# The router's logits: tokens streamed past 32-column weights, then a 32x32 transposition on VectorE

## The reference

```python
logits = hidden @ router_w.T                 # [8192, 128] @ [128, 16]
top_vals, top_idx = jax.lax.top_k(logits, K) # K = 1
scores = sigmoid(top value at its expert, 0 elsewhere)
routed_in = hidden[None, :, :] * scores.T[:, :, None]
```

## Time and profile before

| | |
|---|---|
| device time, median of 3 runs | 510.09 us (509.06 to 510.21) |
| span of the profiled execution | 528.1 us |
| TensorE busy | 497.9 us, 94% |
| VectorE busy | 363.4 us, 69% |
| ScalarE busy | 345.9 us, 66% |
| POOL busy | 347.9 us, 66% |

### The profile page before, as it was taken

One profiled execution on the slowest core, in us unless ns is written; L12 is line 12 of the kernel. 1 busy time (PEld: TensorE's weight loads), 2 busy tenths in 40 slices (PEclk: granted clock), 3 DMA queues, 4 the chain that ended last, 5 costly groups with the idle time before them and its releaser, 6 DMA issues.

```text
span 528.1 us, 10518 instructions
## 1 busy us (share of the span) xinstructions
PE 497.9 (94%) x3101; PEld 406.0 (77%) x3101; DVE 363.4 (69%) x1036; ACT 345.9 (66%) x643; POOL 347.9 (66%) x576
## 2 busy tenths in 40 slices
PE   8889999999999999999999999999998998799984
PEld 7646777877877877878577679888887987799874
DVE  5978889889889889888787888446434433444335
ACT  3777897987987988977789775632534534455321
POOL 6766668778778778785887866635154565556660
PEclk9999999999999999999999999999999899999988
DMA  6015001101101101101010010102877434441009
GB/s 219 2 51 209 20 21 41 60 22 41 60 21 42 60 22 42 50 11 62 12 50 21 21 41 32 41 21 72 204 207 189 137 101 125 129 116 49 30 12 308
DMA packets 33031, 39.32 MB, mean 74 GB/s; under 512 B 4913, under 2 KB 29113, under 8 KB 32720
## 3 DMA queue, kind: packets, MB, share of 16 engines
q1 hardware_dynamic: 26640, 24.97, 16.2%
q0 software_dynamic: 5760, 13.16, 7.2%
q10 hardware_dynamic: 576, 0.52, 0.3%
HBM read 21.68 MB, written 17.93 MB: 75 GB/s over the span
## 4 chain that ended last, share of the span: by engine, by line
PE 61%; DVE 7%; ACT 7%; issue 7%; another core or an unknown queue 7%; POOL 6%; DMA 2%; SPq 1%; ACTq 0%; DVEq 0%; POOLq 0%
PE bank L418 14%; PE bank L411 8%; PE bank L435 4%; PE bank L405 3%; PE bank L426 3%; PE bank L704 2%; PE bank L705 2%; PE bank L534 2%; PE bank L520 2%; PE bank L544 2%; PE bank L530 2%; PE bank L525 2%; PE bank L551 2%; PE bank L577 2%
## 5 line engine op out<-in xcount | busy, mean ns | idle before, releaser
L418 PE MATMUL bank<-hT,wm 128*128 128x256 f32 x512 | 128.7, 390 | 3.4 <-ACT hT L821 2.2
L418 PEld LDWEIGHTS bank<-hT,wm 128*128 128x128 f32 x512 | 94.0, 195 | 21.8 <-ACT hT L821 7.2
L1287 POOL DMA_INDIRECT out<-shared x55 | 53.9, 979 | 47.3 <-DVE shared L1136 32.2
L411 PEld LDWEIGHTS bank<-wm,k 128*128 128x128 f32 x512 | 62.3, 192 | 10.7 <-issue 6.9
L411 PE MATMUL bank<-wm,k 128*128 128x128 f32 x512 | 63.7, 277 | 1.2 <-ACT k L838 0.9
L870 ACT ACTIVATE er<-bank 128x256 f32<-128x256 f32 x40 | 15.2, 383 | 54.9 <-remote 33.1
L1141 DVE TENSOR_TENSOR e<-er,bank 128x256 f32<-128x256 f32 x40 | 16.8, 420 | 31.1 <-ACT er L870 20.3
L1287 POOL DMA_INDIRECT out<-rows x24 | 23.5, 978 | 20.5 <-DVE rows L1136 11.3
L799 ACT ACTIVATE h<-rows,smE 128x128 f32<-128x128 f32 x64 | 26.3, 482 | 12.6 <-POOL smE L1231 12.5
L435 PE MATMUL bank<-wm,actA 128*128 128x128 f32 x240 | 32.8, 280 | 0.0
L435 PEld LDWEIGHTS bank<-wm,actA 128*128 128x128 f32 x240 | 29.3, 192 | 0.2
(11 more groups left out here) (258 smaller groups left out, 1401.6 us busy)
## 6 DMA issues: line engine op xcount, KB each, us to landing
shared<-sorted_rows SPq DMA_DIRECT2D x56, 128.5 KB
shared<-x SPq DMA_DIRECT2D x16, 256.0 KB
rows<-sorted_rows SPq DMA_DIRECT2D x24, 128.5 KB
wexp<-w_exp SPq DMA_DIRECT2D x2, 1536.0 KB, 9.6
sorted_rows<-filler SPq DMA_DIRECT2D x17, 128.5 KB
shared<-out SPq DMA_DIRECT2D x6, 256.0 KB
out<-shared SPq DMA_DIRECT2D x12, 128.0 KB, 2.3
sorted_rows<-rows,posi POOLq DMA_INDIRECT x64
```

Source lines behind the costliest of these rows:

```text
L411: ins = mm(grp(acc, g), grp(lhs, g), W(name, f), start=(f == 0 and g == 0), stop=(f == F // P - 1), skip_group_check=True)
L418: ins = mm(dst[:, j * HALF:(j + 1) * HALF], W(name, 2 * pair_ + j), src[:, half * HALF:(half + 1) * HALF], start=True, stop=True)
L1287: g_.indirect_dma_start(out, bass.IndirectOffsetOnAxis(xr[k % RING][:, j, D:D + 1].bitcast(U32), 0), xr[k % RING][:, j, D + 1:ROW], None, ...
```

## The change

- The router's weights are padded from 16 to RW = 32 columns with zeros (on the host), and become the loaded operand.
- Per tile there are 4 matmuls as before, now one for each quarter c of the array's columns. Each loads the same 128x32 weights into its own 32 columns, streams 128 tokens past them (from each of the 4 groups the 32 tokens c*32 to c*32+31) and writes the PSUM partitions c*32 to c*32+31. The result LGT has 128 partitions (quarter and expert) by 128 columns (group and token).
- VectorE transposes LGT in blocks of 32x32 into `lgt` in SBUF. There a token is again on its own partition, with 4 groups of 32 logits, of which 16 are real.
- mx and oh0 read lgt in SBUF in place of LG in PSUM. mx waits for the transposition.

```diff
-               ("router", NE), ("gate", SF), ("up", SF), ("down", SF)):
+               ("router", RW), ("gate", SF), ("up", SF), ("down", SF)):
...
+        lgt = ring("lgt", 2, (G, RW))
...
-        LG = SMALL[:, 0:G * NE].rearrange("p (g e) -> p g e", e=NE)
-        RK5 = SMALL[:, G * NE:(2 * G + 1) * NE].rearrange("p (g e) -> p g e", e=NE)
+        LGT = SMALL[:, 0:P]
+        RK5 = SMALL[:, P:P + (G + 1) * NE].rearrange("p (g e) -> p g e", e=NE)
...
-                    for g in range(G):
-                        ins = mm(LG[:, g, :], grp(hT[t % HR], g), W("router"), start=True, stop=True)
+                    tokens = hT[t % HR][:, :].rearrange("p (g c i) -> p c g i", g=G, c=P // RW)
+                    for c in range(P // RW):
+                        ins = mm(LGT[c * RW:(c + 1) * RW, :].rearrange("e (g i) -> e g i", g=G), W("router"),
+                                 tokens[:, c, :, :], start=True, stop=True)
                     ins.then_inc(s["LG"], 1)
...
                     wait(dve, "LG", t)
+                    v.transpose(lgt[t % 2][:, :, :].rearrange("p g e -> p (g e)"), LGT).then_inc(s["lgt"], 1)
+                    wait(dve, "lgt", t)
                     wait(dve, "ths", t - 2)
-                    v.reduce_max(mx[t % 2][:, :], LG, AX).then_inc(s["mx"], 1)
+                    v.reduce_max(mx[t % 2][:, :], lgt[t % 2][:, :, 0:NE], AX).then_inc(s["mx"], 1)
...
-                    v.tensor_tensor(oh0[t % 2][:, :, :], LG, mx[t % 2][:, :].unsqueeze(2).to_broadcast([P, G, NE]),
+                    v.tensor_tensor(oh0[t % 2][:, :, :], lgt[t % 2][:, :, 0:NE], mx[t % 2][:, :].unsqueeze(2).to_broadcast([P, G, NE]),
                                     ALU.is_equal).then_inc(s["oh0"], 1)
```

More of the change, by code:

```diff
@@ L38 @@
 LN_EPS, WKV_EPS = 1e-5, 1e-8
+RW = 32
 ROW = 2 * D + 1
@@ L70 @@
     kr2=1, k22=1, VAL2=1, K3=1, kr3=1, k23=1, VAL3=1, REC=1, th=1, rv=1, x2=1, agE=2, pE=3, h=1, T4=1,
-    hT=1, LG=1, mx=1, oh0=1, cm=2, oh=1, ths=1, sc=1, hs=1, RK=1, prk=1, reg=1, pmk=1, posf=1,
+    hT=1, LG=1, lgt=1, mx=1, oh0=1, cm=2, oh=1, ths=1, sc=1, hs=1, RK=1, prk=1, reg=1, pmk=1, posf=1,
     posi=1, G0=1, U0=1, sg0=1, ac0=1, G1=1, U1=1, sg1=1, ac1=1, D1=1, base=1, hG0=1, hU0=1, hsg0=1, hac0=1,
@@ L1314 @@
         "Wkey": a["attn_Wkey"].T, "Wrec": a["attn_Wrec"].T, "Wval": chunks(a["attn_Wval"].T),
-        "router": a["ffn_router_w"].T, "gate": a["ffn_shared_gate_w"].T, "up": a["ffn_shared_up_w"].T,
+        "router": np.pad(a["ffn_router_w"].T, ((0, 0), (0, RW - NE))), "gate": a["ffn_shared_gate_w"].T, "up": a["ffn_shared_up_w"].T,
         "down": chunks(a["ffn_shared_down_w"].T),
```

## The result

The change makes the kernel slightly slower. The changed kernel takes 514.09 us (median of 6 runs, 512.25 to 514.3), the kernel before, run in turn with it, 509.97 (6 runs, 509.06 to 510.48). The ratio of the runs is 1.0058, with a 95% interval of 1.0035 to 1.0081: some 3 us, with 1.8 and 4.1 as the ends of the interval. The forecast was 512.4.

A forecast was written before the change was run, and what follows sets the result against it. A closed loop through VectorE (stA to reciprocal), POOL and the x load was taken as the bound. +2.2 us in 8 turns and +0.1 in three later tiles, +2.3 on 510.09, gave 512.4 us, range 508.0 to 516.0.

The forecast's parts named there:

- Rival 1: TensorE is the real pace maker and gains: 507.2 us, or 503.6 with the larger saving; chance 0.14.
- The transposition: On VectorE between stA and the reciprocal L1093: adds 0.32 us a tile, bounds 0.20 and 0.93.
- Nothing comes back: On VectorE, reduce_max and the first comparison save no time by reading SBUF in place of PSUM.
- The turn: From stA to stA, 8 times: tight turn 20.16 becomes 20.48 us; 8 x 0.27 = +2.2 us in all.
- TensorE: the failed term: Router matmuls and changes of array shape on TensorE: 0.85 us in place of 0.81, +0.04 a tile.
- the third sum: Router matmuls on TensorE overlap only in program order: 5 slots of 0.11, 0.55 us, -0.26 a tile.
- the two tails: On TensorE, the 0.15 us tail behind the last record, taken twice for the changes of array shape: 0.30.
- The second sum: Router matmuls on TensorE run all four column tiles at once: 2 x 0.11 = 0.22 us, -0.59 a tile.
- Behind the turns: After 220 us: three router tiles in the chain, 3 x 0.04 = +0.1 us, bounds -1.8 and +2.3.
- Rival 2: Both cancel: transposition nearer 0.2, TensorE saves 0.26 in three tiles, turns lengthen by 0.15: 510.5 us; chance 0.20.
- Rival 3: TensorE slower: array empties at both changes, column tiles don't overlap, +0.75 a tile: 518.3 us, half of it 514.5; chance 0.14.
- Rival 4: On TensorE, no overlap but no tail either, +0.07 a tile: the forecast's time; chance 0.52 together with the forecast.

The follow-up runs named there:

- experiment 3: Kernel before with the router's column tiles but no transposition; VectorE reads the untransposed logits, so the output differs: 531.13 us, ratio 0.9961 to before.
- experiment 4: Kernel before with its old router matmuls, plus a transposition in front of mx whose result nobody reads: 536.12 us, ratio 1.0049 to before.
- experiment 8: Changed kernel with each of the 4 router matmuls done twice, 16 records in place of 8: 513.77 us, ratio 1.0053 to before.
- experiment 5: Changed kernel with the transposition moved ahead of stA, where VectorE waits for x: 510.07 us, ratio 0.999 to before.
- experiment 10: Changed kernel with four x buffers, transposition ahead of stA, and POOL's smE step put ahead of its rows step: 511.52 us, ratio 1.002 to before.
- 9: Changed kernel with five x buffers in place of four and POOL's smE step put ahead of its rows step: 503.4 us, ratio 0.9873 to before.
- experiment 11: Kernel before with five x buffers in place of four and POOL's smE step put ahead of its rows step: 505.95 us, ratio 0.9934.

## Why the prediction was right, and where it was not

**What bounds the kernel: right, and shown.** The prediction said that the loop stA, reciprocal L1093, POOL, load of x sets the pace, and not TensorE with its 19.96 in 20. TensorE's half alone (experiment 3) leaves the turns at 161.3; VectorE's half alone (4) brings 166.0; 0.24 us more on TensorE (8) cost nothing; the transposition outside the loop (5) costs nothing in the timed runs. The three profiles with the transposition behind stA and four x buffers have turns of 164.8 to 166.0 us, the four without a transposition 161.3 to 162.6. The open end is experiment 5: no profile with four x buffers shows 8 short turns with the transposition ahead of stA (166.3 there, 166.5 in experiment 10), since POOL meets the scan in them, so its lesson rests on the times and on the reciprocal. Rival 1, TensorE as pace maker, falls by its own test: stA goes on waiting for x. It comes true in part once the loop is open (9 against 11).

**The transposition: right.** Forecast 0.32 us, measured slot 0.32, the instruction 0.290 (median of 16). "Nothing comes back" at mx was nearly right: mx takes 0.22 from SBUF against 0.20 from PSUM, so the reciprocal is 0.36 later in place of 0.32.

**The turn: right in the tight turn, too small in the sum.** Tight turns are 20.46 to 20.51, the forecast 20.48. The step that failed is the mean: I took +0.27 for each of 8, since a longer turn would cover the short waits of before. Measured is +3.95 in place of +2.2. The 0.35 up to the issue of the load is there in each turn and makes 2.8. The two late turns of before (0.20 and 0.26) have gone, as the forecast had it, but two others have come, 0.30 where VectorE reaches the scan num late and 0.54 where the power step met the scan: +0.4. The loads make the other +0.8, nearly all of it one load that took 3.6 us; why, stays open, and experiment 4 has a slow load (3.7 us) in the same turn, while experiment 8, with the same loop, has 2.85 there. Which resource the load meets was not tested. Long turns don't need the transposition: the padding alone has two. That the transposition makes them more frequent isn't shown. So +2.8 is the part of the turns that the runs show to be the change's, and the rest of the +3.95 is of the size of the scatter.

**TensorE: the failed term.** Forecast +0.04 a tile, measured -0.34. I took the third sum (program order, five slots of 0.11) and two tails of 0.15. Experiment 8 shows two slots, 0.24, where the third sum had 0.55; that is the term that failed, since column tiles do not wait for one another in the order of the program. All that lies around it comes to 0.23, where I had 0.30 for the two tails: that was nearly right, and the first 0.09 of it stands in front of the router, at the gate product. The second sum, all four at once, was the right one for the matmuls. The Trainium skill, TensorE: Matmul & The Clock Gate, Part 3, has packed tiles start some 4 ns apart: the trace agrees that they run beside one another, with 0.35 us for 8 records of 0.284, but the starts that it shows lie farther apart, an estimated 0.02 us ((0.42 - 0.284) / 7). The skill's TensorEngine Tiling (Array Packing), Key Properties, has a drain at a change of mode: the trace agrees with some cost at the change, 0.09 in front of the router, and all of it is inside the 0.23. In the loop the term has the weight 0, so its error doesn't show in the turns.

**Behind the turns:** forecast +0.1, measured -1.85. A part of this isn't the change's. In the five profiles with the longer second phase, that of before among them, the last prk starts 0.97 to 1.45 us behind the last count on TensorE (L557 before, 360.07 - 359.10 there); in the nine others, the old router matmuls of experiment 11 among them, it is 0.29 (363.02 - 362.73 after). So 0.68 of the 1.85 comes with the execution of before that was profiled, for a reason that isn't known, and about -1.2 is left. Three tiles in the chain at -0.34 are -1.0, inside the bound of -1.8 given. The router's starts show it in part: two of the last three rounds are 18.33 for 18.67 and 14.89 for 15.51. The rounds just behind the turns differ by up to 0.5 between kernels with no reason in this code. The 0.7 of slack in the last tile was not quite enough: TensorE now waits 0.17 for oh there, as it comes sooner itself.

**Rival 2** (both cancel) had the transposition at 0.2; it took 0.29. **Rival 3** (TensorE loses) is excluded by the 0.35. **Rival 4** had no overlap; experiment 8 shows overlap. Its time was the forecast's, so the time could not have told the two apart.

The forecast's +2.3 thus stands near the measured 3 because two errors have opposite signs: the turns are 1.8 more than forecast, what lies behind them 2.0 less, and the start adds 0.85 of scatter. The mechanism was right, and of the number a good part is luck.

## What to carry to other kernels

An engine at 99% busy needn't be the pace maker: look for a joint with a constant wait (here stA for x, POOL for a reciprocal, SyncE for POOL) and follow it once round; if the loop closes in the time of a round, what is saved elsewhere is worth nothing, and what is added inside counts in full. Before placing a new instruction, find the idle time in the loop and put it on that side: here the same transposition cost some 3 us behind stA and nothing ahead of it. When one loop is opened, read the next one in the same profile before judging: the fifth buffer alone made the kernel before 8.6 us slower and left the changed one 6.4 us slower than before, and with one POOL step moved the changed kernel was 1.3%, some 6.5 us, faster than before.

## What the hardware showed that I had not expected

**A scan on VectorE holds POOL.** POOL's power step of smE works on 128x4 numbers and takes 1.03 us when it starts at least 0.19 us before the scan num. In the five rounds, over all traces, in which it started between 0.06 us before the scan and 0.04 behind its start, it took 1.97 to 2.04, and 1.85 in the two in which it started 0.12 behind. The four instructions of rows go from 1.41 to between 2.31 and 2.44 when the scan falls among them, and stay at 1.41 beside the reciprocals, which have one input. The surplus, 0.9 to 1.0, is near the scan's 1.16. It isn't the scan alone: the small copy of rows, 0.19 us in all other rounds of before, took 0.65 in the one in which VectorE's q, again with two inputs in SBUF, ran beside it.

```profile
61.92 0.65 POOL L1212 COPY rows<-id_all 128x4 int32<-128x4 int32 x1
```
```profile
61.84 0.68 DVE L1055 SCALAR_TENSOR_TENSOR q<-den,er 128x512 f32<-128x512 f32 x1
```

The Trainium skill, SBUF — State Buffer, Who interferes with whom, describes a port pair that VectorE and GpSimd share as an exclusive lock, over which a VectorE instruction with two inputs in SBUF contends with a GpSimd instruction that reads SBUF: the trace agrees, since the scan reads decay and ev from there, and q reads den and er. A shift of 0.2 us between two engines that have no semaphore between them can so cost 1 us.

**Column tiles of 32 overlap though each matmul is two records:** 0.35 us for 8 records of 128 columns, 0.59 for 16. The change of array shape, there and back, costs no more than some 0.23 us in all, 0.09 of it at the product in front.
